# An LSTM-over-graph kernel: the last layer's bias is added to X on VectorE instead of through a selector matmul on TensorE

## The reference

```python
h = relu(layernorm(x))
x = x + L0(h)          # two graph layers, then four skips of an LSTM
h = relu(layernorm(x))
x = x + L1(h)
# L0: h = relu(adj @ (h @ Wg0 + bg0)); h = relu(adj @ (h @ Wg1 + bg1))
#     for p in 1..4: windows of p steps through an LSTM, the last hidden state replaces step p-1 of each window
# L1: for k, a in enumerate((diag(adj), triu(adj, 1), tril(adj, -1))): out += a @ (h @ W[k]);  out += bias
```

## Time and profile before

| | |
|---|---|
| median of 3 runs | 428.75 us (428.46 to 430.12) |
| the profiled execution's own time | 432.43 us |
| its span, first to last instruction | 429.2 us |
| TensorE matmul busy | 407.1 us, 95% |
| VectorE busy | 328.3 us, 76% |
| ScalarE busy | 282.3 us, 66% |
| GpSimd busy | 47.2 us, 11% |
| mean granted TensorE clock | 0.984 of full |

### The profile page before, as it was taken

How to read it: one execution, slowest core, us unless ns; L and a number is a source line. 1 busy time by engine, 2 the same in 40 slices (tenths; PEclk the granted TensorE clock), 3 DMA queues, 4 the chain that set the end, 5 groups by cost and what they waited for, 6 DMA issues and landing times.

```text
span 429.2 us, 7735 instructions
## 1 busy us (share of the span) xinstructions
PE 407.1 (95%) x2562; PEld 365.1 (85%) x2562; DVE 328.3 (76%) x843; ACT 282.3 (66%) x568; POOL 47.2 (11%) x55
## 2 busy tenths in 40 slices
PE   3997989899999999999989999999999999999897
PEld 2785879898878889999867889999887789999787
DVE  5478788897877688887977678878888777767841
ACT  4676556766875666767675666777586676757542
POOL 3791002000300002000110000200120000000300
PEclk9996989899999999999999999999999999999999
DMA  7900000000001000000000100000000000000011
GB/s 219 370 26 1 0 2 0 2 2 0 2 1 39 31 2 12 3 20 1 2 2 18 37 12 12 1 18 0 1 0 21 25 2 12 2 18 2 2 61 61
DMA packets 6079, 11.14 MB, mean 26 GB/s; under 512 B 1056, under 2 KB 4768, under 8 KB 5536
## 3 DMA queue, kind: packets, MB, share of 16 engines
q1 hardware_dynamic: 6048, 10.77, 7.1%
HBM read 6.57 MB, written 4.19 MB: 25 GB/s over the span
## 4 chain that ended last, share of the span: by engine, by line
PE 83%; DVE 9%; ACT 4%; issue 3%; POOL 1%; DMA 1%; DVEq 0%; ACTq 0%; POOLq 0%
PE PS L459 12%; PE PS L455 12%; PE PS L456 11%; PE PS L513 8%; PE PS L472 6%; PE PS L469 6%; PE PS L468 6%; PE PS L496 5%; PE PS L392 4%; PE PS L411 3%; PE PS L403 3%; PE PS L421 2%; ACT GT L685 2%; PE PS L482 1%; ACT TC L694 1%
## 5 line engine op out<-in xcount | busy, mean ns | idle before, releaser
L685 ACT ACTIVATE GT<-PS,BG 128x256 f32<-128x256 f32 (+2 forms) x312 | 159.7, 563 | 59.3 <-PE PS L472 33.9
L455 PE MATMUL PS<-HH,WIH 128*128 128x256 f32 (+2 forms) x312 | 111.1, 356 | 7.4 <-DVE HH L831 3.6
L459 PE MATMUL PS<-HL,WIH 128*128 128x256 f32 (+2 forms) x312 | 105.9, 339 | 0.5
L456 PE MATMUL PS<-HH,WIL 128*128 128x256 f32 (+2 forms) x312 | 105.5, 338 | 0.0
L694 ACT ACTIVATE TC<-CS 128x512 f32<-128x512 f32 (+2 forms) x88 | 45.1, 512 | 41.9 <-DVE CS L805 27.8
L455 PEld LDWEIGHTS PS<-HH,WIH 128*128 128x128 f32 x312 | 60.9, 195 | 13.0 <-DVE HH L831 4.3
L459 PEld LDWEIGHTS PS<-HL,WIH 128*128 128x128 f32 x312 | 60.9, 195 | 7.2 <-DVE HL L839 2.6
L318 POOL TENSOR_TENSOR RS<-VE,NHALF 128x8 f32<-128x8 f32 (+2 forms) x15 | 26.5, 1766 | 356.2 <-DVE VE L753 356.2
L456 PEld LDWEIGHTS PS<-HH,WIL 128*128 128x128 f32 x312 | 61.1, 196 | 3.7
L472 PE MATMUL PS<-SL,WHH 128*128 128x256 f32 (+2 forms) x192 | 59.8, 311 | 0.0
L469 PE MATMUL PS<-SH,WHL 128*128 128x256 f32 (+2 forms) x192 | 59.8, 311 | 0.0
(11 more groups left out here) (78 smaller groups left out, 566.9 us busy)
## 6 DMA issues: line engine op xcount, KB each, us to landing
X<-x_tbd SPq DMA_DIRECT2D x3, 1024.0 KB, 12.1
out_tbd<-X SPq DMA_DIRECT2D x15, 192.0 KB, 1.9
X<-x_tbd SPq DMA_DIRECT2D x4, 256.0 KB, 4.3
WI<-wih_t SPq DMA_DIRECT2D x1, 1024.0 KB, 6.5
out_tbd<-X SPq DMA_DIRECT2D x7, 128.0 KB, 1.7
WH<-whh_t SPq DMA_DIRECT2D x1, 768.0 KB, 7.8
out_tbd<-X SPq DMA_DIRECT2D x1, 256.0 KB, 2.0
WL<-w_l SPq DMA_DIRECT2D x1, 192.0 KB, 7.3
```

Source lines behind the costliest of these rows:

```text
L455: pe.matmul(dst, WIH[:, p - 1, cols], x_high, start=True, stop=False)
L456: pe.matmul(dst, WIL[:, p - 1, cols], x_high, start=False, stop=False)
L459: mm = pe.matmul(dst, WIH[:, p - 1, cols], x_low, start=False, stop=(j == 0))
L685: act.activation(GT[:, s, q, 0:n], bank(s, q)[:, 0:n], ACT.Tanh if q == C else ACT.Sigmoid, bias=BG[:, 4 * (p - 1) + q:4 * (p - 1) + q + 1 ...
```

## The change

TensorE's bias matmul (line 508), its operands TWO, BIASH and BIAS2 and their preparation on GpSimd go. The first of the three matmul pairs of a batch now starts the sum itself. A new function `add_bias` on VectorE adds BIAS, broadcast over 8 batches, to X of the group in two instructions, one for each stream. In the groups' units it stands behind unit 1's low part (`BIAS_AT = 1`), in the last group behind `split_h3`. It waits for the H3 of the first 8 batches, which ScalarE makes from X; the other 8 are made by VectorE, earlier in its own order. The add of chunk 0 waits for both additions to be complete. VectorE waits for the late weights, of which BIAS is one, once at its start.

```diff
--- before.py
+++ after.py
@@ -103,7 +103,7 @@
 TAIL = range(LATE.chunks[-1][0], G)
 
 
-NORM_AT, SPLIT_AT = 0, 2
+NORM_AT, BIAS_AT, SPLIT_AT = 0, 1, 2
 
 CELL_EARLY = (1, 2, 15)
 
@@ -167,9 +167,6 @@
         BG0T = sb("BG0T", [D, T])
         BG1 = sb("BG1", [T, D])
         BIAS = sb("BIAS", [T, D])
-        BIASH = sb("BIASH", [T, D], F32R)
-        BIAS2 = sb("BIAS2", [T, D], F32R)
-        TWO = sb("TWO", [T, T], F32R)
         BI = sb("BI", [D, 16])
         BH = sb("BH", [D, 16])
         BG = sb("BG", [D, 16])
@@ -235,7 +232,7 @@
         h3_first = sem("h3_first")
         h3_high = sem("h3_high")
         h3_second = sem("h3_second")
-        bias_parts = sem("bias_parts")
+        x_biased = sem("x_biased")
         uk_mm = sem("uk_mm")
         uk_sb = sem("uk_sb")
         out_mm = sem("out_mm")
@@ -354,16 +351,6 @@
             pool.wait_ge(consts, 8)
             pool.tensor_tensor(ADJ3L[:, :, :], ADJ3[:, :, :], ADJ3H[:, :, :].bitcast(F32),
                                ALU.subtract).then_inc(consts, 1)
-            pool.wait_ge(w_late, 32)
-
-
-            pool.memset(TWO[:, :].bitcast(F32), 0.0).then_inc(bias_parts, 1)
-            pool.tensor_copy(BIASH[:, :], BIAS[:, :]).then_inc(bias_parts, 1)
-            pool.wait_ge(bias_parts, 2)
-            pool.memset(TWO[0:2, :].bitcast(F32), 1.0).then_inc(bias_parts, 1)
-            pool.tensor_tensor(BIAS2[:, :], BIAS[:, :], BIASH[:, :].bitcast(F32), ALU.subtract).then_inc(bias_parts, 1)
-            pool.wait_ge(bias_parts, 4)
-            pool.tensor_copy(BIAS2[0:1, :], BIASH[0:1, :].bitcast(F32)).then_inc(bias_parts, 1)
 
             def group(i, more):
                 if more:
@@ -502,16 +489,10 @@
             def last_out(g, n, ps, plan):
 
                 c, first, last = chunk_of(plan, n)
-                if first:
-
-                    size = plan.chunks[c][1]
-                    pe.matmul(as_batches(ps)[:, 0:size, :], TWO[:, :],
-                              BIAS2[:, :].unsqueeze(1).broadcast_to([T, size, D]), start=True, stop=False,
-                              skip_group_check=True)
                 pe.wait_ge(uk_sb, G * g + n + 1)
                 for k in range(ADJ_PARTS):
                     mm = pe.matmul(as_batches(ps)[:, n - plan.chunks[c][0], :], UK[:, n % 4, k * T:(k + 1) * T],
-                                   WL1[:, k, :], start=False, stop=(k == ADJ_PARTS - 1), skip_group_check=True)
+                                   WL1[:, k, :], start=(k == 0), stop=(k == ADJ_PARTS - 1))
                 if last:
                     mm.then_inc(out_mm, 1)
 
@@ -572,7 +553,6 @@
             units(0, None)
             pe.wait_ge(consts, 9)
             pe.wait_ge(w_late, 32)
-            pe.wait_ge(bias_parts, 5)
             next_graph(0)
             with pe.Fori(1, GROUPS - 1) as i:
                 units(i, STEADY)
@@ -873,10 +853,21 @@
                                          in1=H3H[:, :, :].bitcast(F32),
                                          op0=ALU.max, op1=ALU.subtract).then_inc(h3_second, 1)
 
+            def add_bias(g):
+
+                dve.wait_ge(h3_first, HB * g + HB)
+                for s in range(STREAMS):
+                    part = bass.ds(g * G + s * HB, HB)
+                    dve.tensor_tensor(X[:, part, :], X[:, part, :],
+                                      BIAS[:, :].unsqueeze(1).broadcast_to([T, HB, D]),
+                                      ALU.add).then_inc(x_biased, 1)
+
             def add_out(g, c, ps, plan):
 
                 first, size = plan.chunks[c]
                 dve.wait_ge(out_mm, CHUNKS * g + c + 1)
+                if c == 0:
+                    wait_apart(dve, x_biased, STREAMS * g + STREAMS, x_quarter[0], 16)
                 part = bass.ds(g * G + first, size)
                 dve.tensor_tensor(X[:, part, :], as_batches(ps)[:, 0:size, :], X[:, part, :],
                                   ALU.add).then_inc(out_ready, 1)
@@ -895,6 +886,7 @@
                 part(0, 0)
                 part(1, 0)
             dve.wait_ge(x_rest, 16 * (GROUPS - 1))
+            dve.wait_ge(w_late, 32)
 
             def units(i, more, plan):
                 for k in range(len(UNITS)):
@@ -917,6 +909,8 @@
                     unit_low(k, i)
                     if plan and k == NORM_AT:
                         norm_h3(i - 1)
+                    if plan and k == BIAS_AT:
+                        add_bias(i - 1)
                     if plan and k == SPLIT_AT:
                         split_h3(i - 1)
 
@@ -950,6 +944,7 @@
             add_out(i - 1, CHUNKS - 1, bank(1, 3), LATE)
             norm_h3(i)
             split_h3(i)
+            add_bias(i)
             out_ring = [bank(0, 0), bank(0, 1), bank(1, 0), bank(1, 1)]
             for c in range(CHUNKS):
                 add_out(i, c, out_ring[c % 4], STEADY)
```

## The result

The changed kernel takes 437.01 us, the median of four runs (435.61 to 441.81), where the kernel before took 428.61 in four runs. The ratio is 1.0199 with a 95% interval of 1.0155 to 1.0244: slower, by 8.4 us between the medians. A later series beside 23 runs of the kernel before gave 435.29 against 428.71, a ratio of 1.0174 (1.0119 to 1.0229). The forecast was 435.8, in a range of 432.0 to 438.2.

A forecast was written before the change was run, and what follows sets the result against it. TensorE was taken to bound the kernel, its matmuls busy for 95% of the span. Delays of 3 x 2.2 less 2.5 spared gave +4.1, clock falls +3.0: 428.75 + 7.1 = 435.8 us, range 432.0 to 438.2.

The forecast's parts named there:

- The hole: TensorE at batch 3, waiting for VectorE's add of chunk 0: idle about 2.4 us, +2.2 us a group, three times.
- the sum: Span change before the clock: three delays of 2.2 us less 2.5 us spared on TensorE, +4.1 us.
- Nothing taken back: Later in each group, TensorE's waits move with its own results, so none of the 2.2 us delay is recovered.
- No second delay: VectorE behind the additions has just caught up by CS(3), 235.4 against gates at 236.0, so no further delay.
- What TensorE is spared: Removed bias matmuls: 3.8 us by their steps, of which 2.5 us comes through.
- The tail's 0.96: After 405 us the chain is TensorE's own, so the removed matmuls there save 0.96 us.
- chunk 0's nothing: Chunk 0's matmul in groups 1 to 3: its 0.18 us goes into following waits, saving nothing.
- The clock: TensorE's clock falls behind the new holes: 1.5 us each, two falls likeliest, +3.0 us.
- The tail's additions: In the last group the additions delay chunk 0's add, but TensorE wants its bank only later: zero cost.
- the cheap additions: Rival: additions at line 870's pace, delay 1.1 us a group, +0.8 us, 429.6 us; chance 0.07.
- the hole made good: Rival: TensorE's hole at batch 3 is refilled by later waits, leaving only the removal, 425.7 us; chance 0.05.
- The clock that holds: Rival: same delay with no fall or one, 432.8 or 434.3 us; chances 0.13 and 0.22.

The follow-up runs named there:

- the additions alone: Kernel before with its bias matmuls kept and the 8 additions put in at the change's places, adding a tile of zeros: 439.54 us, ratio 1.024.
- no bias at all: Changed kernel with neither the 24 matmuls nor the 8 additions: 426.36 us against 428.92 for the kernel before, ratio 0.9926.

## Why the prediction was right, point by point

- **The hole: right.** The additions took 1.22 us (1.23 put), the hole was 2.42 us (2.4), the piece of batch 3 came 2.23 us late (2.2). Another 0.1 was not in the sum: the first matmul behind a hole takes 0.21 us to the next where others take 0.11. Its weight load starts only at 231.40, the matmul itself at 231.41. 2.33 in all.
- **Nothing taken back: right**, shown by the additions alone: 2.5 us in each of three groups.
- **No second delay: right.** In groups 1 and 3, where the clock held, VectorE idled 0.73 us ahead of CS(3), waiting for its gates (0.6 put). The 2.35 us in the rows of group 2 are longer because those gates were made at half clock. So VectorE had little to spare.
- **What TensorE is spared: too high,** and this is the term that was mis-sized. I put 0.60, 0.60 and 0.36 us for chunks 2 to 5; they gave 0.25, 0.25 and 0.07. I had looked for a wait behind chunk 0's matmul and behind the LATE group's last, but took chunks 4 and 5 at full step. Behind both stands a wait for VectorE's HH or ScalarE's GT, at the start of skip 3 and of skip 4. The rows that said so were in the chain before: it leaves TensorE for ScalarE and VectorE there. The tail's 0.96 came out at 0.94, chunk 0's nothing at nothing.
- So the change without the clock is +5.5 in the span, not +4.1: 1.0 less spared and 0.4 more delay. The 0.4 saved outside the span was not in the sum either.
- **The clock: right in kind and size.** 1.5 us a fall was put and 1.5 to 1.6 measured for the changed kernel; two more falls were put as likeliest, 1.7 is the mean. In the profiles four of nine holes had one, fewer than the two in three of the forecast. It was a guess on the number, from two cases (the same trace has a third, with the longest hole but the one at its start, 3.16 us up to 36.51, and 6.8 us at half clock from 35.76, which the forecast left out), and the forecast owes its closeness to it: with the sum corrected to 5.5 the forecast would have been 437.3, 0.3 from the first series and 2.0 from the second. That 435.8 came so near is luck in part: the sum was 1.4 us too low, and half of that was made good by some 0.3 us too much for the falls and by the 0.4 us outside the span.
- The tail's additions cost nothing, as put: VectorE still idles 2.41 us behind the first adds there.
- Of the rivals, the cheap additions and the hole made good fell with the first two points. The clock that holds is one end of what the executions show, not the middle.

## What to carry to other kernels

Work moved to a less busy engine is priced by what stands behind it in that engine's order. Against no bias at all the same eight additions cost 7.5 us of the span, falls apart, ahead of an add that hands a PSUM bank back, and 0.6 us a few units later, where mostly the store waits. Before costing a removed instruction at its step, look at the next wait on its engine: if another engine sets it, the step comes back as idle time. And a hole in TensorE's work costs a second time where the clock falls behind it: one of 1.2 us cost its length alone, one of 2.4 us often 1.6 us more. Whether two short holes are cheaper than a long one was not tried.

## What the runs showed of the hardware that was not expected

- A two-input addition of 128x1024 f32 on GpSimd takes 2.35 to 2.63 us and holds up VectorE's instructions on SBUF beside it, a one-input cast included (2.47 us for 0.43), until it ends. The Trainium skill (GPSIMD Engine Reference, "Specifications") says that GpSimd shares its SBUF interfaces with VectorE, with contention for instructions with two SBUF inputs or in a two-port mode; the trace agrees, and shows that the contention can be a full stop.
- All 23 stretches at half clock within the ten profiled spans began between 0.75 us before and 1.5 us after the end of a hole of 1.65 us or more in TensorE's work; none stood at one of the holes of 1.03 to 1.48 us. The same hole can have a fall in one execution and none in another: that of 1.99 us in the first group had one in six of the ten profiles, that of 1.65 us in four.
- Holes of 2.4 us in TensorE's work were followed by 3.4 us at 1.2 GHz in four of the nine cases in the profiles of the change (two executions) and of the additions alone; holes of 1.2 us in none of three, and eleven of twelve executions with such holes have no more than the usual two falls. What decides among holes of the same length is not shown here.
- The kernel's own spread, 426.7 to 432.5 us before, goes for the most part with the number of falls, 0 to 4 by the mean clock; in its one profiled execution all four are in the first group.
